# Attention and routing kernel: x read once into a ring of five batches, with the adds, zeros and one low half moved to match

## The chip, the cores and the metric

The kernel runs on one core of one Trainium2 chip. The metric is device time in microseconds (us), from start to end of one execution; less is better. The core has TensorE (PE, matrix products, with PEld for loading its weights), VectorE (DVE), ScalarE (ACT), GpSimd (POOL) and SyncE (SP), which here issues nearly all the DMAs, all on one queue. Each engine takes its instructions in order and waits on semaphores for the others.

## What is computed

16 batches of 1024 rows of 256 numbers are normalized; from these come an attention with a feature map (elu + 1) instead of a softmax and 16 heads, and a mixture of 8 experts in which each expert takes its 256 best rows of a batch. Both are added to x.

```python
x = L0_attn_x                       # 16 x 1024 x 256
xn = _layernorm(x, axis=-1)
# attention
Q = elu(xn @ Wq.T + bq) + 1;  K = elu(xn @ Wk.T + bk) + 1;  V = xn @ Wv.T + bv
KV = einsum('bshd,bshe->bhde', K, V)
Z = 1.0 / (einsum('bshd,bhd->bsh', Q, K.sum(axis=1)) + 1e-06)
out = einsum('bshd,bhde,bsh->bshe', Q, KV, Z).reshape(b, s, E) @ Wo.T + bo
# experts
probs = softmax(einsum('ntd,de->nte', xn, gate_w)).transpose(0, 2, 1)
g, m = jax.lax.top_k(probs, 256)
h = einsum('nekf,efd->nekd', gelu(einsum('nekd,edf->nekf', xn[m], w1)), w2)
ffn = zeros.at[m].add(g[..., None] * h).astype(bfloat16)
x = x + out + ffn
```

## The kernel before

The program has two parts. The first goes over the 16 batches: statistics, normalized rows, keys, queries, sums, the attention's output, and the gate. It leaves in memory the normalized rows in 16-bit halves (table), x plus attention (mix) and an array of zeros (acc) for the experts' sums. The second part gathers rows from table for each expert, multiplies by w1 and w2 and adds the results into acc; at its end acc is added to mix. The change touches the first part alone.

In the first part body n of each engine's program has eight slots, j = 0 to 7, one for each tile of 128 rows. In body n the keys and queries of batch n are made, and with a lag of two bodies (LAG) the output of batch m = n - 2.

- **SyncE** loads x of batch n + 2 into xring, which holds 3 batches (L601), and x of batch m + 1 a second time into x2ring, which holds 2 (L612). The second copy is where the output is summed. It also issues the DMA transposes of the normalized halves xhl into xT, one for each tile (turn, L558), of which tiles 4 to 7 of batch n and 0 to 3 of batch n + 1 are issued in body n; the rows for table (L569); the rows of mix (store_mix, L580); the weights that are scanned for their largest value (pieces, batches 2 to 9); and the zeros for acc (clear, L585), 16 of 1 MB, two in each of the bodies 8 to 15. A transpose waits for the low half of its tile.
- **VectorE** takes the statistics of x (L930), their moments for batch n + 1 in slot 3 (L946), the low halves of xhl (low, L1025), the feature map of the keys (k_feature, L1065), the reciprocals of Z and their splitting into three 16-bit parts (L1082 to L1092), the sum of output and x2ring (add_x, L1105), and in batches 5 to 15 the search for the 256 best of each expert (L254 to L262).
- **ScalarE** makes the high halves (L825), the exponentials and phk, the high half of the keys (key_high, L837).
- **GpSimd** makes, in this order in a slot: the centred tiles xm (centre, L733), phk's low half (key_low, L744) of the tile before, the bias bo added to two tiles of x2ring (add_bo, L759), in slots 1, 2, 5 and 6 for batch m. In slot 3 come the variance for batch n + 1 (norm, L722, after VectorE's moments), then key_low of tile 2 and the power -1/2 (root, L726), on which the centres of batch n + 1 depend. After the last body it has the adds of batches 14 and 15.
- **TensorE** projects a tile to its keys and logits (project, L1317 to L1322), sums keys times rows (sum_kv, L1335 and L1339, needs both halves of phk), projects the queries (L1356), makes denominators (L1368), spreads the reciprocals (L1389) and forms the output (L1404). In body 1 it multiplies the blocks of bv with Wo once (bias_blocks, L1307), from kvT, which VectorE writes at L1019.

The raw weights lie at the start in xring's third batch, and the raw bias of the keys in x2ring's second. The order is that in which each engine's program is written out; there is no scheduler.

## Time and profile before

| | us |
|---|---|
| median of three runs | 1897.31 |
| lowest, highest | 1896.3, 1904.78 |
| the profiled execution | 1902.01 |
| its span, first to last instruction | 1900.3 |

Mean granted clock of TensorE over the span: 0.990 of full speed. The first part ends, and the experts begin, at 545.73 us. The views are of one execution. The view by stretches gives for a stretch each engine's busy time with its number of instructions, the granted TensorE clock (1.00 is 2.4 GHz, 0.50 is 1.2 GHz), the share of the 16 DMA engines in use and the rate. A batch begins there where TensorE projects its first tile. In the timeline a row is an instruction or several alike: start, length, engine, line, operation, what it writes and reads, count, and in brackets the engine's idle time before it and what ended that.

### The profile page before, as it was taken

The page shows a single profiled execution, that of the slowest core. Times are in us where ns is not written, and L with a number is a line of the kernel's source. Part 1 is how long each engine was busy: PE and PEld are TensorE (multiplying, and loading weights), DVE is VectorE, ACT ScalarE, POOL GpSimd, SP SyncE. Part 2 cuts the span into 40 slices and gives each one's busy share as a digit, 9 for nine tenths or more (in the row PEclk, how much of TensorE's full clock was granted, in tenths as well). Part 3 has the DMA queues.
Part 4 walks back from the last instruction along what each step waited for, and adds up shares of the span by engine and source line. Part 5 has one row for each costly group of instructions (what it writes and reads, how often), then busy time and mean ns, then how long its engine had stood idle before and what let it go on. Part 6 is the DMA issues. An engine that isn't in the chain of part 4 may idle for free.

```text
span 1900.3 us, 39708 instructions
## 1 busy us (share of the span) xinstructions
PE 1836.1 (97%) x13916; PEld 1290.6 (68%) x13916; DVE 1294.9 (68%) x2569; ACT 1246.6 (66%) x2014; POOL 1104.5 (58%) x981
## 2 busy tenths in 40 slices
PE   5899998998999999999999999999999999999998
PEld 3577776776776666666666666666666666666666
DVE  6678997998857777745787875555555555555556
ACT  5788887776636666666666666666666666666665
POOL 6678786878535554655455555545554555555453
PEclk8999999999999999999999999999999999999999
DMA  6689899899755655575767667676766767676657
GB/s 167 165 238 257 238 249 265 227 255 236 206 166 124 131 122 120 139 187 143 172 151 187 154 159 181 134 179 157 185 155 158 172 137 184 154 186 156 179 124 222
DMA packets 449187, 338.26 MB, mean 178 GB/s; under 512 B 225043, under 2 KB 430614, under 8 KB 449046
## 3 DMA queue, kind: packets, MB, share of 16 engines
q1 hardware_dynamic: 383958, 253.84, 48.5%
q0 software_dynamic: 48864, 66.88, 19.4%
q10 hardware_dynamic: 16224, 15.73, 2.5%
q8 instruction: 79, 1.29, 0.3%
q14 instruction: 62, 0.51, 0.1%
HBM read 185.61 MB, written 100.40 MB: 151 GB/s over the span
## 4 chain that ended last, share of the span: by engine, by line
PE 70%; DMA 1%; DVE 0%; issue 0%; ACT 0%; POOL 0%; SPq 0%; POOLq 0%
PE pY L2005 35%; PE pH L1990 35%; DMA lacc<-acc 1%; DMA acc<-yo,idx 0%; PE pR L300 0%; POOL acc L1764 0%; ACT lffn L1800 0%; DVE yo L1866 0%; PE pN L240 0%; PE pN L284 0%; DVE lmix L1915 0%; DVE fffn L1912 0%; ACT hid L1789 0%; DVE hid L1850 0%; ACT gel L1786 0%
## 5 line engine op out<-in xcount | busy, mean ns | idle before, releaser
L2005 PE MATMUL pY<-w2s,hid 128*128 128x256 f16 x6144 | 756.6, 273 | 0.9 <-DVE hid L1850 0.8
L1990 PE MATMUL pH<-xgT,w1s 128*128 128x512 f16 (+1 forms) x3120 | 747.7, 376 | 1.3 <-PEq L329 1.3
L2005 PEld LDWEIGHTS pY<-w2s,hid 128*128 128x128 f16 x6144 | 599.7, 98 | 180.8 <-DVE yo L1866 3.6
L1764 POOL DMA_INDIRECT acc<-yo,idx x254 | 407.0, 1602 | 515.7 <-DVE yo L1866 442.7
L1850 DVE SCALAR_TENSOR_TENSOR hid<-gel,cur,hid 128x512 f16<-128x512 f32 (+1 forms) x520 | 384.6, 740 | 446.4 <-ACT hid L1789 345.5
L1786 ACT ACTIVATE gel<-pH,cur 128x512 f32<-128x512 f32 (+1 forms) x520 | 353.9, 681 | 481.5 <-PE pH L1990 405.7
L1990 PEld LDWEIGHTS pH<-xgT,w1s 128*128 128x128 f16 x3120 | 305.2, 98 | 252.3 <-DMA xgT<-xg 1.6
L1789 ACT ACTIVATE hid<-gel,cur 128x512 f16<-128x512 f32 (+1 forms) x520 | 372.0, 715 | 17.1
L224 POOL DMA_INDIRECT xg<-table,idx x256 | 292.3, 1142 | 112.1 <-issue 59.3
L733 POOL TENSOR_SCALAR xm<-xring,moments,rpow 128x256 f32<-128x256 f32 x128 | 163.9, 1281 | 2.0 <-DVE xhl L1025 0.4
L744 POOL TENSOR_TENSOR phk<-phik,phk 128x256 f16<-128x256 f32 x128 | 93.0, 727 | 108.6 <-ACT phk L837 107.4
L1866 DVE TENSOR_SCALAR yo<-pY,gains,cur 128x256 f32<-128x256 f32 x256 | 121.6, 537 | 14.6 <-PE pY L2005 13.0
L1339 PE MATMUL pKV<-phk,xhl 128*128 128x256 f16 x768 | 105.6, 275 | 0.0
L1356 PE MATMUL pQ<-xT,wq 128*128 128x512 f16 x384 | 94.2, 382 | 4.6 <-ACT qraw L844 4.5
L213 DVE SCALAR_TENSOR_TENSOR w1s<-stage,cur,w1s 128x1024 f16<-128x1024 f32 x64 | 83.0, 1296 | 17.8 <-ACT w1s L205 14.4
L213 DVE SCALAR_TENSOR_TENSOR w2s<-stage,cur,w2s 128x1024 f16<-128x1024 f32 x64 | 82.2, 1285 | 17.8 <-ACT w2s L205 12.9
L759 POOL TENSOR_TENSOR x2ring<-x2ring,bo_all 128x512 f32<-128x512 f32 x64 | 87.1, 1364 | 0.0
L825 ACT ACTIVATE xhl<-xm 128x256 f16<-128x256 f32 x128 | 52.5, 411 | 50.4 <-POOL xm L733 48.8
L1025 DVE TENSOR_TENSOR xhl<-xm,xhl 128x256 f16<-128x256 f32 x128 | 74.8, 585 | 6.4 <-ACT xhl L825 6.4
L830 ACT ACTIVATE ek<-pP,winv_neg 128x256 f32<-128x256 f32 x128 | 59.8, 467 | 25.4 <-PE pP L1322 25.2
L1317 PE MATMUL pP<-wkg,xT 128*128 128x272 f16 x256 | 52.0, 286 | 23.8 <-DMA xT<-xhl 16.6
L205 ACT ACTIVATE w1s<-stage,cur 128x1024 f16<-128x1024 f32 x64 | 72.5, 1133 | 0.0
(247 smaller groups left out, 1991.5 us busy)
## 6 DMA issues: line engine op xcount, KB each, us to landing
stage<-in_w SPq DMA_DIRECT2D x160, 512.0 KB, 5.0
xring<-in_x SPq DMA_DIRECT2D x16, 1024.0 KB, 7.1
x2ring<-in_x SPq DMA_DIRECT2D x16, 1024.0 KB, 7.8
table<-xhl SPq DMA_DIRECT2D x32, 512.0 KB, 4.7
mix<-x2ring SPq DMA_DIRECT2D x32, 512.0 KB
acc<-zeros SPq DMA_DIRECT2D x16, 1024.0 KB, 5.1
fmix<-mix SPq DMA_DIRECT2D x48, 256.0 KB
facc<-acc SPq DMA_DIRECT2D x48, 256.0 KB
```

The costliest lines, as they stand in the source:

```text
L213: nc.vector.scalar_tensor_tensor(out=part_dst(i, 1, r), in0=staged(r), scalar=cur[i][:, 2 + r // 2:3 + r // 2], in1=part_dst(i, 0, r), op0 ...
L224: nc.gpsimd.indirect_dma_start(xg[i][:, s, :, :, :].rearrange("p a c t -> p (a c t)"), None, table, bass.IndirectOffsetOnAxis(ap=idx[q % 4 ...
L733: g.tensor_scalar(xm[:, j % HALF, :], xring[:, n % XR, j, :], moments[:, j, 0:1], rpow[:, j:j + 1], ALU.subtract, ALU.mult).then_inc(xm_do ...
L1339: last = t.matmul(pKV[:, c * D:(c + 1) * D], xhl[h][:, jj, a, c, :], phk[:, j % 4, b, :], start=j == 0 and k == 0 and c == 0, stop=j == NT ...
L1356: last = t.matmul(pQ[:, :], wq[:, b, cc, c * P:(c + 1) * P], xT[h][:, a, cc, :], start=k == 0 and cc == 0, stop=k == 2 and cc == DC - 1)
L1764: g.indirect_dma_start(acc, bass.IndirectOffsetOnAxis(ap=idx[q][:, s:s + 1], axis=0), yo[i][:, s, :], None, compute_op=ALU.add).then_inc(a ...
L1786: a.activation(gel[:, hc % 2, w], pH[hc % 4][:, w], ACT.Gelu_apprx_tanh, scale=c[:, 0:1]).then_inc(gel_done, 1)
L1789: a.activation(hid[:, hc % 4, 0, w], gel[:, hc % 2, w], ACT.Copy, scale=c[:, 1:2]).then_inc(hhi_done, 1)
L1850: v.scalar_tensor_tensor(out=hid[:, hc % 4, 1, w], in0=gel[:, hc % 2, w], scalar=cur[expert_of(b, q)][:, 1:2], in1=hid[:, hc % 4, 0, w], o ...
L1866: last = v.tensor_scalar(yo[i][:, s, :], pY[s // 2][:, s % 2, :], gains[:, ds(column_of(b * 4 + quarter_of(b, q)) * 4 + s, 1)], cur[expert ...
L1990: last = t.matmul(pH[hc % 4][:, tok], w[:, aw, c, hc * P:(hc + 1) * P], xgT[i][:, ad, c, tok], start=k == 0 and c == 0, stop=k == 2 and c ...
L2005: last = t.matmul(pY[s // 2][:, s % 2, :], hid[:, hc % 4, ad, s * P:(s + 1) * P], w[:, aw, hc, :], start=hc == 0 and k == 0 and s % 2 == 0 ...
```

## The change

xring gets five batches and x2ring goes. Batch n lies in slot (n + 4) % 5, so that batch 15, which is stored in the second part, keeps the place that it had in memory. x is loaded once; the load of batch n + 2 stands after the transpose of tile 5, where the second load stood, and waits for the stored rows of batch n - 3. The bias is added in body n to batch n itself, two bodies earlier than before, in slots 2, 5, 6 and 7 instead of 1, 2, 5 and 6, and no adds stand behind the last body. The zeros of bodies 8 and 9 go to bodies 0 and 1. In slot 3 the low half of tile 2 stands ahead of the variance. The products of bv and Wo go from slot 0 to slot 4 of body 1 on TensorE (and from 1 to 5 on ScalarE), and the small constants of `offsets` from body 1 to body 3 on VectorE. Every line number behind the edits shifts by some lines, 5 to 10.

```diff
     LAG = 2
-    XR = 3
+    XR = 5
...
             xring = sb("xring", [P, XR, NT, D], F32)
-            x2ring = sb("x2ring", [P, 2, NT, D], F32)
+
+            def slot(n):
+
+                return (n + XR - 1) % XR
...
-                sp.dma_start(xring[:, 1, :, :], x_rows[1]).then_inc(x_in, 16)
-                sp.dma_start(x2ring[:, 0, :, :], x_rows[0]).then_inc(x2_in, 16)
+                sp.dma_start(xring[:, slot(1), :, :], x_rows[1]).then_inc(x_in, 16)
...
-                def body(n, s1, s2, load, load2, scan, ahead, wipe, nxt):
+                def body(n, s1, s2, load, scan, ahead, wipe, nxt):
                     m = n - LAG
                     if s1:
                         turn(n, HALF)
                         store_rows(n, 0)
+                    if s1:
+                        turn(n, HALF + 1)
                     if load:
                         value = held(sp, at(x_in, n, 1))
                         sp.wait_ge(consts, 1)
                         sp.wait_ge(x_in, value)
-                        value = held(sp, at(xm_done, n, -1))
-                        sp.wait_ge(consts, 1)
-                        sp.wait_ge(xm_done, value)
-                        sp.dma_start(xring[:, (n + 2) % XR, :, :], x_rows[ds(n + 2, 1)].rearrange("o p j d -> p (o j) d")).then_inc(x_in, 16)
-                    if s1:
-                        turn(n, HALF + 1)
-                    if load2:
-                        value = held(sp, at(x2_in, m))
-                        sp.wait_ge(consts, 1)
-                        sp.wait_ge(x2_in, value)
-                        for h in range(2):
-                            value = held(sp, at(mix_out[h], m, -1))
-                            sp.wait_ge(consts, 1)
-                            sp.wait_ge(mix_out[h], value)
-                        sp.dma_start(x2ring[:, ds((m + 1) % 2, 1), :, :].rearrange("p o j d -> p (o j) d"),
-                                     x_rows[ds(m + 1, 1)].rearrange("o p j d -> p (o j) d")).then_inc(x2_in, 16)
+                        if s2:
+                            for h in range(2):
+                                value = held(sp, at(mix_out[h], m, -1))
+                                sp.wait_ge(consts, 1)
+                                sp.wait_ge(mix_out[h], value)
+                        sp.dma_start(xring[:, ds(slot(n + 2), 1), :, :].rearrange("p o j d -> p (o j) d"),
+                                     x_rows[ds(n + 2, 1)].rearrange("o p j d -> p (o j) d")).then_inc(x_in, 16)
...
                     if wipe:
-                        clear(2 * n - NB)
+                        clear(2 * n if isinstance(n, int) and n < LAG else 2 * n - NB)
...
                 def add_bo(m, u):
 
-                    pool.wait_ge(x2_in, at(x2_in, m))
-                    tiles = x2ring[:, ds(m % 2, 1), 2 * u:2 * u + 2, :].rearrange("p o j d -> p (o j) d")
+                    pool.wait_ge(x_in, at(x_in, m))
+                    tiles = xring[:, slot(m), 2 * u:2 * u + 2, :]
...
-                        if nxt and j == HALF - 1:
-                            norm(n + 1)
                         if nxt and j > HALF:
                             centre(n + 1, j - (HALF - 1))
                         if j > 0:
                             key_low(n, j - 1)
                         elif n > 0:
                             key_low(n - 1, NT - 1)
                         if nxt and j == HALF - 1:
+                            norm(n + 1)
                             root(n + 1)
                         if nxt and j in (HALF - 1, HALF):
                             centre(n + 1, j - (HALF - 1))
-                        if n >= LAG and j in (1, 2, 5, 6):
-                            add_bo(n - LAG, (1, 2, 5, 6).index(j))
+                        if j in (2, 5, 6, 7):
+                            add_bo(n, (2, 5, 6, 7).index(j))
                         if n > 0 and j == HALF:
                             sums_of(n - 1)
                 key_low(NB - 1, NT - 1)
-                for u in range(4):
-                    add_bo(NB - LAG, u)
                 sums_of(NB - 1)
...
                 gather(pool, 0, 0, 0)
-                for u in range(4):
-                    add_bo(NB - 1, u)
...
-                    if n == 1:
+                    if n == LAG + 1:
                         offsets()
...
-                        if n == 1 and j == 0:
-                            bias_blocks()
                         if j in (2, 3):
                             q_part(n, j - 2)
+                        if n == 1 and j == 4:
+                            bias_blocks()
```

On SyncE, the stretch from the transpose of tile 4 in body 9: L601 is the load into xring, L612 the one into x2ring; before:

```order
L558 DMA_TRANSPOSE xT<-xhl 128x4x128
L569 DMA table<-xhl 128x4x512
L601 DMA xring<-in_x 128x8x256
L558 DMA_TRANSPOSE xT<-xhl 128x4x128
L612 DMA x2ring<-in_x 128x8x256
L558 DMA_TRANSPOSE xT<-xhl 128x4x128 x2
L569 DMA table<-xhl 128x4x512
L547 DMA stage<-in_w 128x1024
L547 DMA stage<-in_w 128x4x256
L558 DMA_TRANSPOSE xT<-xhl 128x4x128 x2
```

and now:

```order
L560 DMA_TRANSPOSE xT<-xhl 128x4x128
L571 DMA table<-xhl 128x4x512
L560 DMA_TRANSPOSE xT<-xhl 128x4x128
L607 DMA xring<-in_x 128x8x256
L560 DMA_TRANSPOSE xT<-xhl 128x4x128 x2
L571 DMA table<-xhl 128x4x512
L549 DMA stage<-in_w 128x1024
L549 DMA stage<-in_w 128x4x256
L560 DMA_TRANSPOSE xT<-xhl 128x4x128 x3
```

The load of x2ring is gone, and the one of xring (L607 now) stands behind the second transpose of the stretch, that of tile 5. The zeros (L585) that followed the transpose of tile 1 aren't in this body any more.

On SyncE the bodies 0 and 1, from the transposes of batch 1's tiles on, before:

```order
L558 DMA_TRANSPOSE xT<-xhl 128x4x128 x3
L569 DMA table<-xhl 128x4x512
L558 DMA_TRANSPOSE xT<-xhl 128x4x128 x5
L569 DMA table<-xhl 128x4x512
L601 DMA xring<-in_x 128x8x256
L558 DMA_TRANSPOSE xT<-xhl 128x4x128 x3
L569 DMA table<-xhl 128x4x512
L558 DMA_TRANSPOSE xT<-xhl 128x4x128 x4
L547 DMA stage<-in_w 128x1024
```

and now:

```order
L560 DMA_TRANSPOSE xT<-xhl 128x4x128 x2
L571 DMA table<-xhl 128x4x512
L560 DMA_TRANSPOSE xT<-xhl 128x4x128 x2
L587 DMA acc<-zeros 128x8x256
L560 DMA_TRANSPOSE xT<-xhl 128x4x128 x2
L587 DMA acc<-zeros 128x8x256
L560 DMA_TRANSPOSE xT<-xhl 128x4x128
L571 DMA table<-xhl 128x4x512
L560 DMA_TRANSPOSE xT<-xhl 128x4x128
L607 DMA xring<-in_x 128x8x256
```

The zeros (acc, L587 now) stand between transposes of batches 1 and 2.

On GpSimd, slots 0 to 3 of a body from batch 2 on. xm is a centred tile, phk a low half of the keys, veps the variance, rpow the power; before:

```order
L733 TENSOR_SCALAR xm<-xring,moments,rpow 128x256
L744 TENSOR_TENSOR phk<-phik,phk 128x256
L733 TENSOR_SCALAR xm<-xring,moments,rpow 128x256
L744 TENSOR_TENSOR phk<-phik,phk 128x256
L759 TENSOR_TENSOR x2ring<-x2ring,bo_all 128x512
L733 TENSOR_SCALAR xm<-xring,moments,rpow 128x256
L744 TENSOR_TENSOR phk<-phik,phk 128x256
L759 TENSOR_TENSOR x2ring<-x2ring,bo_all 128x512
L722 TENSOR_SCALAR veps<-moments 128x8
L744 TENSOR_TENSOR phk<-phik,phk 128x256
L726 TENSOR_TENSOR rpow<-veps,minus_half 128x8
L733 TENSOR_SCALAR xm<-xring,moments,rpow 128x256
```

and now:

```order
L754 TENSOR_TENSOR xring<-xring,bo_all 128x512
L728 TENSOR_SCALAR xm<-xring,moments,rpow 128x256
L739 TENSOR_TENSOR phk<-phik,phk 128x256
L728 TENSOR_SCALAR xm<-xring,moments,rpow 128x256
L739 TENSOR_TENSOR phk<-phik,phk 128x256
L728 TENSOR_SCALAR xm<-xring,moments,rpow 128x256
L739 TENSOR_TENSOR phk<-phik,phk 128x256
L754 TENSOR_TENSOR xring<-xring,bo_all 128x512
L739 TENSOR_TENSOR phk<-phik,phk 128x256
L717 TENSOR_SCALAR veps<-moments 128x8
L721 TENSOR_TENSOR rpow<-veps,minus_half 128x8
L728 TENSOR_SCALAR xm<-xring,moments,rpow 128x256
```

An add has gone from slot 1 to the end of the body before, ahead of the low half of the last tile there, and in slot 3 the low half of tile 2 stands ahead of the variance.

## Rows read from the trace of the kernel before

**Rows 1.** The page: busy time and share of each engine; a group of instructions.
```profile
PE 1836.1 (97%) x13916; PEld 1290.6 (68%) x13916; DVE 1294.9 (68%) x2569; ACT 1246.6 (66%) x2014; POOL 1104.5 (58%) x981
...
L759 POOL TENSOR_TENSOR x2ring<-x2ring,bo_all 128x512 f32<-128x512 f32 x64 | 87.1, 1364 | 0.0
```
**Rows 2.** Stretches, from:to length, then PE, PEld, DVE, ACT, POOL busy, clock, DMA.
```profile
44.05:75.96 31.91, 22.53 (x167) 14.92 (x165) 17.08 (x64) 22.32 (x51) 19.01 (x21) 0.89 0.40 102
...
137.01:166.28 29.27, 29.27 (x289) 23.24 (x288) 23.74 (x60) 25.52 (x57) 23.30 (x24) 1.00 0.88 251
...
196.95:227.11 30.16, 29.19 (x285) 22.55 (x284) 28.16 (x74) 25.66 (x57) 24.13 (x24) 1.00 0.92 245
...
287.43:324.77 37.34, 32.18 (x286) 24.30 (x284) 28.06 (x75) 25.88 (x57) 23.49 (x24) 0.91 0.93 257
...
385.21:417.56 32.35, 29.77 (x287) 22.77 (x286) 30.30 (x84) 21.71 (x48) 25.07 (x24) 1.00 1.04 235
...
448.34:480.88 32.54, 29.18 (x286) 22.54 (x285) 27.00 (x70) 21.85 (x48) 23.87 (x24) 1.00 0.94 260
...
509.80:545.73 35.93, 30.62 (x281) 25.32 (x281) 23.01 (x47) 3.29 (x7) 15.41 (x17) 0.86 0.34 103
545.73:1900.30 1354.57, 1346.39 (x9328) 914.10 (x9328) 850.49 (x1390) 858.16 (x1168) 711.85 (x571) 1.00 0.66 160
...
515.80:526.00 10.20, 8.99 (x66) 7.29 (x67) 5.72 (x10) 0.00 (x0) 0.00 (x0) 0.50 0.46 156
```
**Rows 3.** TensorE's waits from 80 to 500 us: in total, times, longest.
```profile
PE pP L1317 <- DMA xT<-xhl: 13.6, 10, 2.7
PE pS L1335 <- POOL phk L744: 8.3, 9, 1.0
```
**Rows 4.** Timeline of SyncE's queue in batch 9 (the two loads of x).
```profile
296.05 0.42 SPq L601 DMA_DIRECT2D xring<-in_x  x1
...
299.16 0.40 SPq L612 DMA_DIRECT2D x2ring<-in_x  x1
299.66 5.88 SPq L558 DMA_TRANSPOSE xT<-xhl  x2
```
**Rows 5.** The page's DMA issues: count, size of each, median us to landing.
```profile
xring<-in_x SPq DMA_DIRECT2D x16, 1024.0 KB, 7.1
x2ring<-in_x SPq DMA_DIRECT2D x16, 1024.0 KB, 7.8
...
acc<-zeros SPq DMA_DIRECT2D x16, 1024.0 KB, 5.1
```
**Rows 6.** Timeline of TensorE in batch 9, the projection of tile 6.
```profile
308.67 0.64 PE L1317 MATMUL pP<-wkg,xT 128*128 128x272 f16 x2 [2.72 <-DMA xT<-xhl]
```
**Rows 7.** Timeline of GpSimd in batch 8, slots 0 and 3.
```profile
260.07 0.67 POOL L744 TENSOR_TENSOR phk<-phik,phk 128x256 f16<-128x256 f32 x1 [3.82 <-ACT phk L837]
...
269.38 0.81 POOL L722 TENSOR_SCALAR veps<-moments 128x8 f32<-128x8 f32 x1 [1.36 <-DVE moments L946]
270.27 0.67 POOL L744 TENSOR_TENSOR phk<-phik,phk 128x256 f16<-128x256 f32 x1
```
**Rows 8.** Timeline in batch 1: VectorE's kvT and TensorE's products with it.
```profile
48.03 0.47 DVE L1019 TENSOR_SCALAR kvT<-head_mask,bvT 128x128 f32<-128x128 f32 x2
...
48.56 0.80 PE L1307 MATMUL pD<-woT,kvT 128*128 128x256 f32 x1 [3.56 <-DVE kvT L1019]
```
**Rows 9.** Timeline in the tail, GpSimd, VectorE and TensorE.
```profile
510.22 4.99 POOL L759 TENSOR_TENSOR x2ring<-x2ring,bo_all 128x512 f32<-128x512 f32 x4
...
512.83 1.26 DVE L1088 TENSOR_TENSOR zrest<-zz,zpart 128x128 f32<-128x128 f32 x1
514.12 1.17 DVE L1090 CAST zpart<-zrest 128x128 bf16<-128x128 f32 x1
...
516.60 0.80 PE L1420 MATMUL pP<-woT,kvT 128*128 128x256 f32 x1 [3.21 <-DVE kvT L1070]
...
529.58 0.36 DVE L1088 TENSOR_TENSOR zrest<-zz,zpart 128x128 f32<-128x128 f32 x1
```

47 lines of the change are left out of this document (23 added, 24 removed).

## The prediction

> **What bounds the kernel now.** I read the views in this order: busy time, stretches between batch starts, waits, and the timeline of what stands around each wait. TensorE is busy for 97% of the span [rows 1]. The stretches show two parts. From 545.73 us to the end are the experts: TensorE is busy for 1346.39 of 1354.57 us there at full clock [rows 2], and no edited instruction stands there, so I take its time as fixed. The edits all lie in the 545.73 us before it, the attention part, 16 batches long.
>
> In batch 4 (137.01 to 166.28) TensorE is busy for all 29.27 us: that is TensorE's own work for a batch, the floor. Batches 2 to 14 reach from 75.96 to 480.88, 404.92 us for 13 batches, and 13 floors are 380.5. So 24.4 us stand above the floor. Three things fill them: waits of the K projection (L1317) for a transpose from the DMA queue, 13.6 us in 10 waits; waits of the K sums (L1335) for GpSimd's low half phk, 8.3 us in 9 [rows 3]; and batch 9, where TensorE was busy for 32.18 us at a granted clock of 0.91 against 29.2 elsewhere [rows 2], 3.0 us for a stretch at 1.2 GHz after its waits. The sum, 24.9, agrees with 24.4. Batch 1 and the tail (509.80 to 545.73) have losses of their own. VectorE is nearly as full: 28.16 of 30.16 us in batch 6 [rows 2].
>
> **The loads of x.** The change takes out 16 loads of 1 MB, as many as it keeps; the kept ones take 7.1 us from issue to landing, the removed 7.8 [rows 5]. Before, the queue of batch 9 held load, transpose 5, second load, transposes 6 and 7, the two loads 3.1 us apart [rows 4]: 2 MB are asked for in 3 us and need some 11. Transpose 6 is issued right behind the second load and its projection waited 2.72 us [rows 6]. Now transpose 5 goes ahead of the one load that is left, and transpose 6 stands behind 1 MB instead of 2. The load takes the place of the second one, about 3 us later than the first was issued, so transpose 6 lands about 7.4 (what a load takes) minus 3.1 = 4 us earlier relative to its projection. The largest wait is 2.72, so nearly all ten go. Two exceptions: zeros now go out in batches 0 and 1, two of their transfers (5.1 us each, [rows 5]) just before batch 2, which has a wait of this kind; and batch 14 has four weight loads ahead of a transpose, untouched by the change. For the two I keep 3 us. Bounds for the term: 0 (below) and 13.6; taken 10.6. Batches 8 and 9 also lose their four zero writes, which collided there with loads and the scan, so the low clock of batch 9 goes: 3.0, all or nothing.
>
> The x load now also waits for the stored rows of the batch three back. SP waited for that in the same place before, for the second load, so nothing new is queued behind it. VectorE wants this x only in slot 7, five slots of some 3.7 us later (29.3 us have eight), and the load takes 7.1 [rows 5]: cost 0, and it would need a delay of over 10 us to cost anything.
>
> **The third tile's low half.** In batch 8, GpSimd waited for VectorE's moments until 269.38, did the variance and only then the low half at 270.27 to 270.94, for which TensorE was waiting [rows 7]. With the low half first it runs about 1.2 us earlier, since its input was there; the wait for moments moves behind it, where the next centre stands, and this has slots of slack because the next batch's first transposes land long before use. TensorE's 8.3 us go. What is late next is VectorE: at a period of 29.27 its 28.16 us leave 1.1 us for its own waits, where it had 2.0 [rows 2]. Bounds 0 and 8.3; I take 6, nearer the upper end because batch 4 ran at the floor with VectorE and GpSimd in the same order [rows 2].
>
> **The bias adds.** 64 adds of 1.36 us stay 64. In the steady batches three stand about where they were; the fourth goes from the second slot to the end of the batch before, ahead of the low half of tile 7. GpSimd sat idle for 3.82 us just before that one [rows 7], which covers 1.4; cost 0 there, 1.4 a batch if that cover were gone. Removing it from slot 1 frees nothing that is waited for. The eight adds of batches 0 and 1, new there, are 10.9 us of GpSimd work beside TensorE's; batch 1 leaves it 31.91 - 19.01 = 12.9 us idle [rows 2]. Bounds: 0 and some 4 if they push the centres; taken 1.
>
> **The head.** In batch 1 TensorE waited 3.56 us for kvT, which VectorE wrote only at 48.03 behind the offsets and statistics, and then did the four products at half clock [rows 8]. The products go four slots later and the offsets two batches on, so the wait goes. Batch 1 is a chain of short waits of all engines (TensorE 22.53 of 31.91 busy), so part is given back: bounds 1 and 5.5, taken 4. The zeros now go through the queue here, at a DMA share of 0.40 [rows 2]; four transfers of 5.1 us in front of transposes: bounds 0 and 10, taken 1.
>
> **The tail.** Before, four adds (510.22 to 515.21) ran on GpSimd while VectorE split the reciprocals: one step took 1.26 us and the next 1.17, where the first took 0.36 later with GpSimd quiet. TensorE waited 3.21 us behind them [rows 9]. These adds are gone from here: 2.0 us (bounds 1 and 2.2). The Trainium skill, "SBUF — State Buffer", section "Who interferes with whom", says that a VectorE instruction with two SBUF inputs and a GpSimd one that reads SBUF block each other for a whole instruction; by this rule the step grew by waiting for an add, and the trace agrees. Then the clock: 515.80 to 526.00 ran at 0.50, 1.2 GHz, with TensorE busy for 8.99 us [rows 2]; half of that, 4.5, comes back if it doesn't fall. With the wait down to about 1.2 us it is like batch 12, whose waits left the clock at 1.00 [rows 2], more than like batch 9. Bounds 0 and 4.5, taken 3 since VectorE's chain runs beside it. The four adds at the very end lay behind TensorE's work: 0.
>
> **The sum.** 10.6 + 3.0 + 6 + 4 + 2 + 3 = 28.6 saved, 2 spent: 26.6. The profiled execution took 1902.0 us (its span 1900.3 and 1.7 around it), 4.7 above the median of the runs, 1897.3. From 1902.0 the sum gives 1875.4; from the median 1870.7. Part of the 4.7 will be waits of the kind that go, part not: I take 1873.
>
> **The rivals.**
> 1. VectorE becomes the bound. For it: 28.16 of 30.16 us busy in batch 6, 30.30 in batch 12. Against: half of VectorE's 2.0 us of idle time is enough for the floor. If the period stays near 30.1 in the nine batches 5 to 13, the 6 us are not gained and some 3 of the DMA term: 1873 + 9 = 1882. The Trainium skill's page "SBUF — State Buffer", by the rule above, gives it a reason: adds that have moved by a slot or two meet other two-input steps of VectorE. What that would give is this same case.
> 2. The wait changes its name: transpose 6 still stands behind a load, and if this is late because SP comes to it late, the term of 10.6 and the 3.0 stay: 1873 + 13.6 = 1887. Against: 4 us of relief against waits of at most 2.72.
> 3. All goes: upper bounds throughout (13.6 + 3 + 8.3 + 5.5 + 2.2 + 4.5 = 37) and less than nothing spent: 1862.
> 4. Slower. The four zero writes ahead of transposes in batches 0 to 2 each hold a projection for their 5.1 us, and TensorE falls to 1.2 GHz after each, 3 us a time as in batch 9: 32 us, against a gain that is cut to 20 because batch 1's goes too: 1897 + 12 = 1909. It decides from the point where those transposes have under 5 us of slack. Against: a DMA share of 0.40 in batch 1.
>
> **Chances.** Forecast (1866 to 1880) 0.56; rival 1 0.17; rival 2 0.12; rival 3 0.09; rival 4 0.06. A measurement here can tell about 0.5% from no change, which is 9.5 us: faster is below 1887.8. Forecast, rivals 1 and 3 and part of rival 2 lie there: 0.83; within 0.11, slower 0.06. The range from 1862 to 1889 leaves out rival 4, the far side of rivals 2 and 3, and no more.
>
> **What would show it.** In the profile of the changed kernel: waits of L1317's successor for xT below 4 us in 80 to 500 us, no wait of the K sums for phk, batches 6 to 8 at 29.3 to 29.6 us, batch 9 no longer than its neighbours, the products of the bias with no wait in batch 1, the reciprocal's splitting step at 0.36 us in the tail and a clock of 1.00 after it, and the start of the experts near 519 us. If batches 6 to 8 still take 30 us, VectorE was the bound; if batches 0 to 2 have grown, the zeros or the early adds cost more than I allowed; if the experts' part moves by more than 1 us, my first step was wrong.

## The result and the profile after

The changed kernel takes 1883.74 us (median of 4 runs, 1881.06 to 1884.64), the kernel before 1899.3 (4 runs, the three of "Time and profile before" and one more). The ratio is 0.9913 with a 95% interval from 0.9886 to 0.9939. It is faster. The time lies in the range of 1862 to 1889 us, but outside the 1866 to 1880 to which the forecast itself gave 0.56, and nearest to rival 1's 1882. The gain is 15.6 us in the medians. In the profiled executions, from which the sum was made, it is 18.7 us where the sum gave 26.6: the span went from 1900.3 to 1881.6 us.

The stretches of the changed kernel answer to [rows 2]. The columns are the same: from:to, length, then the busy time of TensorE, its weight loads, VectorE, ScalarE and GpSimd, the granted clock, the DMA share and GB/s. In order: batches 0 and 1, batches 6, 7, 9 and 14, batch 15 with the tail, batches 2 to 14 together, the experts, and 6.8 us in batch 1. The last line is batches 2 to 14 of the kernel before.

```profile
19.41:75.00 55.59, 41.90 (x305) 27.14 (x306) 32.90 (x91) 41.58 (x94) 45.26 (x45) 0.84 0.72 176
...
193.00:222.61 29.61, 29.18 (x286) 22.54 (x285) 27.77 (x74) 25.49 (x57) 24.17 (x25) 1.00 0.74 213
222.61:252.54 29.93, 29.34 (x286) 22.38 (x284) 28.07 (x75) 25.43 (x58) 24.72 (x25) 1.00 0.82 212
282.47:312.90 30.43, 29.32 (x286) 22.56 (x284) 28.51 (x76) 25.63 (x58) 25.45 (x25) 1.00 0.80 211
...
434.62:468.18 33.56, 30.74 (x286) 23.50 (x285) 27.63 (x72) 21.60 (x48) 24.70 (x25) 0.95 0.85 231
468.18:526.84 58.66, 55.30 (x565) 44.77 (x564) 46.05 (x103) 27.56 (x55) 22.66 (x25) 1.00 0.49 144
75.00:468.18 393.18, 381.63 (x3702) 295.13 (x3700) 348.95 (x936) 311.88 (x690) 315.37 (x313) 1.00 0.81 211
...
526.84:1881.60 1354.76, 1346.38 (x9328) 914.11 (x9328) 851.36 (x1390) 858.00 (x1168) 710.66 (x571) 1.00 0.66 160
67.50:74.30 6.80, 4.03 (x19) 2.00 (x20) 3.68 (x9) 4.69 (x9) 6.27 (x7) 0.50 0.64 186
...
75.96:480.88 404.92, 382.64 (x3702) 296.31 (x3700) 352.39 (x923) 313.83 (x689) 310.90 (x312) 0.99 0.93 247
```

Laid beside the kernel before, stage by stage (us; the third column is what the prediction's terms make of the first):

| stage | before | after | by the prediction |
|---|---|---|---|
| up to batch 0 | 19.8 | 19.4 | 19.8 |
| batches 0 and 1 | 56.2 | 55.6 | 54.2 |
| batches 2 to 14 | 404.9 | 393.2 | 385.3 |
| batch 15 and the tail | 64.9 | 58.7 | 59.9 |
| experts | 1354.6 | 1354.8 | 1354.6 |

The missing 7.9 us lie in batches 2 to 14; batches 0 and 1 fell short by 1.4 more, and the tail and the start made that up. In batches 2 to 14 TensorE's idle time went from 22.3 to 11.6 us (length less busy time), which is 10.7 less where 16.6 was forecast, and its busy time fell by 1.0 instead of 3.0. The two shortfalls, 5.9 and 2.0, are the 7.9. The waits of TensorE there, and those of the first 80 us (what it waited for; total, times, longest), the former to be read beside [rows 3]:

```profile
PE pP L1307 <- DMA xT<-xhl: 5.4, 3, 2.5
PE pS L1325 <- POOL phk L739: 3.6, 8, 0.6
PE pP L1307 <- DVE phik L1055: 2.6, 7, 0.8
```

```profile
PE pQ L1346 <- ACT qraw L834: 8.2, 3, 4.2
```

The waits for transposes fell from 13.6 us to 5.4, and two make up nearly all of that: batch 2 (2.06) and batch 14 (2.51). The waits for the low half phk fell from 8.3 us to 3.6 in 8, not to nothing, and a wait for VectorE's phik that stood at 0.3 is now 2.6. Against the forecast these are 2.4, 1.3 and 2.3 us, together the 6 us of idle time that did not go. The other 2.0 is the clock: batch 9's busy time fell by 2.9 us (32.18 in [rows 2], now 29.32), but batch 14's rose by 1.6 (29.18 and 30.74), at a granted clock of 0.95. In the first 80 us a wait for the queries, qraw, takes 8.2 us. The loads of x land sooner than in [rows 5]:

```profile
xring<-in_x SPq DMA_DIRECT2D x16, 1024.0 KB, 6.0
```

### The profile page after: what moved, and what is told of

Same layout as the page of the kernel before. It is cut to its first block and busy times, and to the rows that moved or that the text cites. A ratio compares the mean times of both kernels' runs of the same rounds, so it can differ in the third digit from the quotient of the medians.

```text
span 1881.6 us, 39627 instructions
## 1 busy us (share of the span) xinstructions
PE 1829.9 (97%) x13916; PEld 1285.1 (68%) x13916; DVE 1289.9 (69%) x2569; ACT 1243.8 (66%) x2014; POOL 1108.2 (59%) x981
## 5 line engine op out<-in xcount | busy, mean ns | idle before, releaser
L739 POOL TENSOR_TENSOR phk<-phik,phk 128x256 f16<-128x256 f32 x128 | 100.0, 781 | 96.5 <-ACT phk L827 96.0
L754 POOL TENSOR_TENSOR xring<-xring,bo_all 128x512 f32<-128x512 f32 x64 | 89.8, 1403 | 0.0
L205 ACT ACTIVATE w2s<-stage,cur 128x1024 f16<-128x1024 f32 x64 | 72.5, 1132 | 0.0
```

The costliest lines, as they stand in the source:

```text
L205: nc.scalar.activation(part_dst(i, 0, r), staged(r), ACT.Copy, scale=cur[i][:, 2 + r // 2:3 + r // 2]).then_inc(whi_done, 1)
```

## The experiments

Each kernel below is the changed kernel with the named edit. The table gives the median and, from the profiled execution, four stages in us, each from one batch's first projection to that of another: batches 0 to 2, 3 to 13, 14, and 15 with the tail up to the experts. The experts take 1354.4 to 1357.1 us in all of them. The kernel before took 1899.55, 1900.1 and 1899.7 us in the three sessions, beside 1899.3 with the changed kernel, so medians of different sessions can be laid side by side to about 1 us. The stages are of one execution each. It lies within 2 us of the kernel's median, but for the kernel before (2.7 above), e5 (1889.56 us, 3.3 above) and e8 (1875.56, 4.3 below). Of the intervals only that of e12 lies clear of the changed kernel's; those of e2, e6, e8 and e10 overlap it, so their gains of 3 to 5 us over the changed kernel are not known to 1 us.

| kernel | median | ratio to before, 95% | 0 to 2 | 3 to 13 | 14 | 15, tail |
|---|---|---|---|---|---|---|
| before | 1899.3 | | 87.7 | 340.8 | 32.5 | 64.9 |
| changed kernel | 1883.74 | 0.9913 [0.9886, 0.9939] | 86.7 | 328.6 | 33.6 | 58.7 |
| e1 ring alone | 1888.89 | 0.9944 [0.9927, 0.996] | 85.3 | 333.1 | 32.1 | 62.0 |
| e2 variance back | 1878.49 | 0.99 [0.9878, 0.9922] | 85.3 | 327.5 | 30.9 | 58.6 |
| e3 zeros back | 1883.56 | 0.9922 [0.9902, 0.9943] | 82.9 | 331.2 | 33.2 | 58.6 |
| e4 adds back | 1887.5 | 0.994 [0.9922, 0.9959] | 82.5 | 333.0 | 33.7 | 62.0 |
| e5 head back | 1886.22 | 0.9925 [0.9904, 0.9947] | 93.2 | 328.6 | 33.5 | 58.2 |
| e6 early adds out | 1880.39 | 0.9897 [0.9873, 0.9921] | 84.1 | 329.5 | 32.8 | 58.2 |
| e7 adds in the tail | 1885.5, one run | | 85.0 | 328.6 | 33.5 | 62.1 |
| e8 adds spread | 1879.83 | 0.9902 [0.9883, 0.9921] | 82.1 | 327.8 | 31.1 | 58.6 |
| e9 queries later | 1885.45 | 0.9929 [0.9907, 0.995] | 88.6 | 329.2 | 33.0 | 58.6 |
| e10 stage loads later | 1878.68 | 0.989 [0.9867, 0.9914] | 85.9 | 328.9 | 30.2 | 58.2 |
| e11 e2 and e8 | 1876.63 | 0.9875 [0.9853, 0.9897] | 85.2 | 326.8 | 31.6 | 58.2 |
| e12 e2, e8 and e10 | 1873.89 | 0.9861 [0.9839, 0.9882] | 84.7 | 326.6 | 29.7 | 58.2 |

**e1: the ring alone.** Everything but the ring of five slots and the single load of x is undone: the variance, the adds, the zeros and the head stand where they stood before. The lines for the zeros and the bias's products are those shown under e3 and e5.

```diff
             for j in range(NT):
...
+                if nxt and j == HALF - 1:
+                    norm(n + 1)
...
-                    norm(n + 1)
...
-                if j in (2, 5, 6, 7):
-                    add_bo(n, (2, 5, 6, 7).index(j))
+                if n >= LAG and j in (1, 2, 5, 6):
+                    add_bo(n - LAG, (1, 2, 5, 6).index(j))
...
+            for u in range(4):
+                add_bo(NB - LAG, u)
...
+            for u in range(4):
+                add_bo(NB - 1, u)
...
-                if n == LAG + 1:
+                if n == 1:
                     offsets()
...
```

> The kernel before with the ring of five and the single load of x alone: adds, zeros, order of the low half and head products where they were. Theory (half of the transposes' waits come from the second load in the queue): batches 2 to 14 fall from 404.9 us to about 396, the batch with scan and zeros together from 37.3 to about 33, and the waits for xT from 13.6 us to about 6; batches 0 and 1 stay at 56 us and the tail (from TensorE's first tile of batch 15 to the experts) at 64.9. Total about 9 us under the kernel before. Rival (the loads weren't the cause, the wait changes its name): batches 2 to 14 stay within 3 us of 404.9.

Measured: 1888.89 us, 10.7 less than before. Batches 2 to 14 went from 404.9 to 394.2, also 10.7. The profiled execution is 13.8 us shorter; the other 3 lie in the tail (62.0 instead of 64.9), where none had been expected. Batch 9 went from 37.34 to 32.24 with the clock at 1.00, although its zeros were still there. In the columns of [rows 2], here are batch 7, batch 9 and batch 15 with the tail, and TensorE's waits from 80 to 484 us:

```profile
222.67:252.82 30.15, 29.18 (x285) 22.65 (x284) 28.43 (x75) 25.63 (x57) 24.14 (x24) 1.00 0.82 210
282.97:315.21 32.24, 29.39 (x286) 22.49 (x284) 28.45 (x75) 25.75 (x57) 23.75 (x24) 1.00 0.98 266
...
469.77:531.73 61.96, 56.68 (x565) 46.00 (x564) 49.47 (x103) 27.56 (x55) 32.31 (x33) 0.97 0.46 136
```

```profile
PE pS L1330 <- POOL phk L739: 8.2, 9, 1.0
PE pP L1312 <- DMA xT<-xhl: 4.8, 2, 3.0
```

The ring carries two thirds of the gain of the whole change. The waits for transposes fell from 13.6 to 4.8, those for phk stayed at 8.2. So the two kinds of wait are separate, and rival 2, by which transpose 6 stays late and the whole term is lost, falls.

**e2: the variance ahead again.** Only the third tile's low half goes back behind the variance.

```diff
+                if nxt and j == HALF - 1:
+                    norm(n + 1)
...
                     key_low(n - 1, NT - 1)
                 if nxt and j == HALF - 1:
-                    norm(n + 1)
                     root(n + 1)
```

> The changed kernel with the variance ahead of tile 2's low half again. Theory (the move gained some 0.4 us a batch where the search for the best runs, since the low half then met VectorE's two-input steps and kept 0.4 to 0.6 us of TensorE's wait): batches 2 to 14 grow from 393.2 us by 4 to 6, TensorE's waits for phk from 3.6 to about 8 us, total 4 to 6 us over the changed kernel. Rival (VectorE is the bound in these batches, so that the wait is free): no change beyond 1 us.

Measured: 1878.49 us, 5.2 under the changed kernel in the median, where 4 to 6 more had been expected. The intervals overlap: that the move, priced at 6 us of gain, gained nothing is surer than that it lost 5. The timeline of GpSimd (start, duration, operation, idle time before it) and of TensorE and VectorE in batch 7 of the changed kernel shows what took its place:

```profile
234.38 1.48 POOL L739 TENSOR_TENSOR phk<-phik,phk 128x256 f16<-128x256 f32 x1 [1.16 <-ACT phk L827]
235.95 0.20 POOL L717 TENSOR_SCALAR veps<-moments 128x8 f32<-128x8 f32 x1
```

```profile
234.34 0.38 DVE L1015 TENSOR_TENSOR xhl<-xm,xhl 128x256 f16<-128x256 f32 x1
234.66 0.67 DVE L1047 TENSOR_TENSOR qring<-qraw,eq 128x512 f32<-128x512 f32 x1
```

```profile
235.92 0.25 PE L1325 MATMUL pS<-one_col,phk 128*128 128x1 f16 x4 [0.59 <-POOL phk L739]
```

And GpSimd and TensorE in batch 7 of e2, with e2's waits from 80 to 484 us:

```profile
234.18 0.67 POOL L739 TENSOR_TENSOR phk<-phik,phk 128x256 f16<-128x256 f32 x1
```

```profile
234.91 0.25 PE L1326 MATMUL pS<-one_col,phk 128*128 128x1 f16 x4 [0.81 <-POOL phk L739]
```

```profile
PE pS L1326 <- POOL phk L739: 5.0, 8, 0.8
PE pP L1308 <- DVE phik L1056: 1.2, 3, 0.6
```

The low half now starts before the variance, but takes 1.48 us instead of the 0.67 of [rows 7], while VectorE does two steps with two inputs from SBUF, the on-chip memory, each; TensorE waits 0.59 us, against 0.81 in e2. In the kernel before the stretched operation was the variance (0.81 in [rows 7], 0.20 here), and the low half behind it was short. GpSimd and VectorE stand in each other's way in this place in both orders. The move only chose who pays. From 80 to 484 us it took 1.4 us from the waits for phk (5.0 to 3.6) and added 1.4 to those for phik (1.2 to 2.6); what makes phik late no run shows. With e1 and e4 this gives batch 7 in four forms, all at full clock (head and zeros, in which e1 and e4 also differ, have no work in batch 7):

| batch 7, us | adds in slots 1, 2, 5, 6 | adds in slots 2, 5, 6, 7 |
|---|---|---|
| variance ahead of the low half | 30.15 (e1) | 29.82 (e2) |
| low half ahead of the variance | 30.27 (e4) | 29.93 (changed) |

```profile
221.53:251.35 29.82, 29.02 (x286) 22.68 (x285) 28.09 (x75) 25.64 (x57) 24.35 (x25) 1.00 0.78 212
```

```profile
220.56:250.83 30.27, 29.49 (x286) 22.40 (x285) 28.42 (x75) 25.43 (x58) 24.66 (x24) 1.00 0.75 209
```

In both columns the new order of low half and variance costs 0.1 us a batch; in both rows the new place of the adds gains 0.33 or 0.34. Over batches 3 to 13 the order costs 1.0 us (327.5 against 328.6). The rest of e2's lead in the profile lies in batches 0 to 2 (1.3 us, within what two executions of the same order differ by there, see the end) and in batch 14 (2.7 us). Batch 14 waits for its transpose in either kernel, but in the changed one the clock falls behind this wait (0.95) and in e2 it doesn't. That is not one execution's luck alone: of the kernels with the stage's loads in their old place the three with the variance ahead (e1, e2, e11) kept the clock at 1.00 there, and of the eight with the other order seven fell to 0.95 (all but e8). What in the order decides this no run shows.

**e4: the adds back.** The bias adds go back to two batches later, in slots 1, 2, 5 and 6 and in the tail.

```diff
-                if j in (2, 5, 6, 7):
-                    add_bo(n, (2, 5, 6, 7).index(j))
+                if n >= LAG and j in (1, 2, 5, 6):
+                    add_bo(n - LAG, (1, 2, 5, 6).index(j))
...
             key_low(NB - 1, NT - 1)
+            for u in range(4):
+                add_bo(NB - LAG, u)
...
+            for u in range(4):
+                add_bo(NB - 1, u)
```

> The changed kernel with the bias adds back at a lag of two batches, in slots 1, 2, 5 and 6 and behind the last body. Theory (the early adds hold up a centre, with it ScalarE's queue and the queries, and TensorE's clock falls): batches 0 and 1 together fall from 55.6 us to about 48, TensorE has no wait of 4 us for qraw there; the tail grows from 58.7 us to about 63, with a splitting step over 1 us and the clock at half after it. Total about the same as the changed kernel, within 4 us. Rival (zeros in the queue are what lengthened batches 0 and 1): batches 0 and 1 stay at 55 us and only the tail grows, total 4 to 6 us slower than the changed kernel.

Measured: 1887.5 us, 3.8 above the changed kernel. Three parts with different signs: batches 0 to 2 are 4.2 us shorter, batches 3 to 13 4.5 longer, the tail 3.3 longer. Batches 0 and 1 fell to 51.4 us, not to 48. The adds cost where they are early and gain in the tail as forecast, and the gain in the steady batches was not in the prediction at all.

**e6: the early adds left out.** It shows the price of the early adds with nothing put in their place; bo is missing from batches 0 and 1 of its output.

```diff
-                if j in (2, 5, 6, 7):
+                if n >= LAG and j in (2, 5, 6, 7):
                     add_bo(n, (2, 5, 6, 7).index(j))
...
-                    dve.wait_ge(bo_done, at(bo_done, m, u))
+                    if m >= LAG:
+                        dve.wait_ge(bo_done, at(bo_done, m - LAG, u))
```

> The changed kernel without the eight bias adds of batches 0 and 1 (bo is left out of these two batches of the output). Theory (early adds): batches 0 and 1 fall from 55.6 us to about 48, nothing else moves, total about 7 us under the changed kernel. Rival (zeros): no change beyond 1 us.

Measured: 1880.39 us, 3.3 less than the changed kernel, half of the 7 that had been expected. Batches 0 and 1 take 50.2 us instead of 55.6; half of that is given back in batch 2 (33.8 us instead of 31.1), where the projection of tile 6 waits 3.18 us for its transpose and the clock falls. In the changed kernel, GpSimd, ScalarE and TensorE in batch 0 look like this:

```profile
37.40 1.45 POOL L754 TENSOR_TENSOR xring<-xring,bo_all 128x512 f32<-128x512 f32 x1
38.84 1.39 POOL L728 TENSOR_SCALAR xm<-xring,moments,rpow 128x256 f32<-128x256 f32 x1
```

```profile
40.26 0.42 ACT L815 ACTIVATE xhl<-xm 128x256 f16<-128x256 f32 x1 [2.06 <-POOL xm L728]
...
41.24 0.77 ACT L834 ACTIVATE qraw<-pQ,bqT_one,winv 128x512 f32<-128x512 f32 x1
```

```profile
42.07 2.74 PE L1346 MATMUL pQ<-xT,wq 128*128 128x512 f16 x6 [3.91 <-ACT qraw L834]
```

The add at 37.40 stands ahead of the centre at 38.84. ScalarE's high half, which needs that centre, waits 2.06 us, the queries stand behind it on ScalarE, and TensorE waits 3.91 us for them, then does the next six products in 2.74 us at half clock (e2's take 1.47 at the same place). The same happened at 70.28 in batch 1, with a wait of 4.17. Not all of this is the adds' doing. Counted from the first projection of batch 0, the queries start after 22.7 us here and 22.5 in e2, which has the same adds, and after 21.5 in e6: an add makes them about 1 us later. In e2 the clock did not fall there, and batches 0 and 1 took 51.6 us. The prediction had seen GpSimd's idle time in batch 1 and not the order inside it.

**e7: adds in the tail.** Four adds of the same size, on data of their own, run on GpSimd where the old ones ran; the rest stays.

```diff
                 key_low(NB - 1, NT - 1)
+                mo_in = spread[:, 0:4, :, :].rearrange("p j c t -> p (j c t)").bitcast(F32).rearrange("p (i d) -> p i d", i=2)
+                for u in range(4):
+                    if u >= 1:
+                        pool.wait_ge(extra_done, at(extra_done, 0, u - 1))
+                    g.tensor_tensor(extra[:, :, :], mo_in, bo_all[:, :].unsqueeze(1).to_broadcast([P, 2, D]), ALU.add).then_inc(extra_done, 1)
```

> The changed kernel with four adds of the same size on GpSimd, of other data into a scratch tile, put back behind the last body, ahead of ksz. Theory (an add and a step of VectorE with two inputs in the on-chip memory hold each other up, and the longer wait of TensorE drops its clock): the steps of splitting take over 1 us instead of 0.3, TensorE waits about 3 us for kvT, the granted clock is 0.5 for 5 to 10 us after it, and the tail grows from 58.7 us by 4 to 6. Rival (the tail gained by the shorter batch 15 alone): the tail grows by less than 1 us.

Measured: 1885.5 us in one run; batch 15 and the tail take 62.1 us instead of 58.7, 3.4 more where 4 to 6 had been expected. VectorE and TensorE in its tail:

```profile
499.13 1.37 DVE L1085 TENSOR_TENSOR zrest<-zz,zpart 128x128 f32<-128x128 f32 x1
500.54 1.24 DVE L1087 CAST zpart<-zrest 128x128 bf16<-128x128 f32 x1
```

```profile
503.09 2.08 PE L1417 MATMUL pP<-woT,kvT 128*128 128x256 f32 x4 [3.52 <-DVE kvT L1067]
```

And in the changed kernel, where the adds are gone:

```profile
499.90 0.29 DVE L1078 TENSOR_TENSOR zrest<-zz,zpart 128x128 f32<-128x128 f32 x1
500.22 0.23 DVE L1080 CAST zpart<-zrest 128x128 bf16<-128x128 f32 x1
```

```profile
501.76 1.13 PE L1410 MATMUL pP<-woT,kvT 128*128 128x256 f32 x4 [1.07 <-DVE kvT L1060]
```

The step zrest takes 1.37 us with the adds beside it and 0.29 without, the cast behind it 1.24 and 0.23, and TensorE waits 3.52 and 1.07 us, as in [rows 9] and as the prediction had it. The Trainium skill, "SBUF — State Buffer", section "Who interferes with whom", says that copies and casts of VectorE, where their operands allow a mode with two ports, can contend with GpSimd as well as steps with two inputs do; the cast's 1.24 against 0.23 us agrees.

**e9: the queries later.** VectorE's q_feature of tile 0 goes from slot 3 to slot 4, away from the third tile's low half. This takes one of the two steps with two inputs out of its way.

```diff
-                if j in (3, 4):
-                    q_feature(n, j - 3)
+                if j == 4:
+                    q_feature(n, 0)
+                    q_feature(n, 1)
```

> The changed kernel with VectorE's first query feature (two inputs in the on-chip memory) one slot later, so that it isn't running when GpSimd makes the low half of tile 2. Theory (the two hold each other up): the low half of tile 2 takes 0.7 to 1.0 us instead of 1.5 in batches 6 to 13, TensorE's wait for it falls from 0.6 to 0.1 us, and batches 6, 7, 8 and 10 come down from 29.6 to 29.9 us to about 29.2, total 2 to 4 us less. Rival (the low half is slow for another reason, or VectorE is the bound): no change beyond 1 us.

Measured: 1885.45 us, 1.7 above the changed kernel where 2 to 4 less had been expected (its batches 0 to 2 are 1.9 us longer), but the place in question changed as the block between the two engines says. GpSimd in batch 7, and the batch:

```profile
238.69 0.88 POOL L739 TENSOR_TENSOR phk<-phik,phk 128x256 f16<-128x256 f32 x1 [1.17 <-ACT phk L827]
```

```profile
227.03:256.58 29.55, 29.20 (x285) 22.39 (x284) 28.04 (x76) 25.33 (x58) 24.09 (x25) 1.00 0.80 214
```

The low half took 0.88 us instead of 1.48, no wait for phk was left in that batch, and batches 6 to 8 took 29.55 to 29.67 us, the upper end of the 29.3 to 29.6 of the prediction; 29.2 had been expected of this run. Over 80 to 484 us the wait for phk is 0.9 us in 1 instead of 3.6 in 8. VectorE had the same work (28.04 us busy), in less time: its load was not the bound, the collision was. The two query steps then stand in a row, with a phik behind them, and that wait grew from 2.6 to 4.3 us:

```profile
PE pP L1308 <- DMA xT<-xhl: 6.7, 4, 2.4
PE pP L1308 <- DVE phik L1055: 4.3, 8, 1.4
PE pS L1326 <- POOL phk L739: 0.9, 1, 0.9
```

The sum of the three waits in this view is 11.9 us, and 11.6 in the changed kernel. The wait for phk fell by 2.7 us, those for phik and for transposes grew by 1.7 and 1.3. This is rival 1's mechanism, by a narrower path than it was written.

**e3: the zeros back.** The four zero writes of batches 0 and 1 go back to batches 8 and 9.

```diff
-                        (0, 1, True, False, True, False, False, True),
-                        (1, LAG, True, False, True, False, True, True),
+                        (0, 1, True, False, True, False, False, False),
+                        (1, LAG, True, False, True, False, True, False),
...
-                        (PIECE_NB, PIECE_NB + 1, True, True, True, True, True, False),
-                        (PIECE_NB + 1, PIECE_NB + SCAN0, True, True, True, True, False, False),
+                        (PIECE_NB, PIECE_NB + 1, True, True, True, True, True, True),
+                        (PIECE_NB + 1, PIECE_NB + SCAN0, True, True, True, True, False, True),
```

> The changed kernel with the four transfers of zeros back in bodies 8 and 9. Theory (zeros cost little in batches 0 and 1 and most of the gain of batch 9 is theirs): batches 0 and 1 shrink by 0 to 1 us, batch 2 by 1 to 2, batch 9 grows from 30.4 by 2 to 4 us; total 0 to 3 us over the changed kernel. Rival (zeros are what lengthened batches 0 and 1): these shrink by 5 us or more and the total falls.

Measured: 1883.56 us, 0.2 off the changed kernel. Batch 2 and batch 9:

```profile
73.47:102.30 28.83, 28.83 (x286) 22.80 (x284) 22.28 (x60) 25.00 (x56) 23.48 (x25) 1.00 0.84 204
278.38:312.08 33.70, 30.96 (x285) 23.57 (x284) 27.90 (x76) 25.70 (x58) 24.98 (x25) 0.95 0.96 254
```

Batch 2 is 2.2 us shorter (28.83 against 31.1), batch 9 3.3 us longer (33.70 against 30.43) with the clock at 0.95. The zeros collide with transposes where they are written, here or there. As stages, batches 0 to 2 are 3.8 us shorter and batches 3 to 13 2.6 longer. The 1.5 us of this that lie in batches 0 and 1 are within what two executions of the same order differ by there. The move of the zeros is worth nothing in the median.

**e5: the head back.** The bias's blocks and products and the offsets go back to the start of batch 1.

```diff
-                        if j == 5 and n == 1:
+                        if j == 1 and n == 1:
                             bias_blocks_out()
...
-                if n == LAG + 1:
+                if n == 1:
                     offsets()
...
+                        if n == 1 and j == 0:
+                            bias_blocks()
                         if j in (2, 3):
                             q_part(n, j - 2)
-                        if n == 1 and j == 4:
-                            bias_blocks()
```

> The changed kernel with its head undone alone: the bias's blocks, their products, their copies and the offsets go back from batches 1 and 3 to the start of batch 1. The step on record gave this 4 us (1 to 5.5). The changed kernel took 55.6 us for batches 0 and 1 and the kernel with the ring alone 56.2, so the gain was not to be seen; with the early adds back at their old place it was (51.4). Theory: the head's gain and the early adds' cost are separate and add up. Then batches 0 and 1 take 59 to 61 us here and the time is 1887 to 1889 us. Rival: in batches 0 and 1 the late queries behind the early adds end last, whatever the bias's products do before them, so the head hides in that wait: batches 0 and 1 at 55 to 57 us, and the time within 1.5 us of the changed kernel's 1883.7.

Measured: 1886.22 us. Batches 0 and 1 take 59.7 us, 4.1 more than in the changed kernel; with batch 2, where the clock falls too, it is 6.5 more. Batches 0 and 1 also take 3.5 us more than in e1 (56.2), which has the same head and no early adds (and no early zeros). That agrees with the theory that head and early adds are separate and add up in that stage; the rival, that the head hides in the wait for queries, falls. In the median the difference is 2.5 us and the intervals of the two kernels overlap, and the profiled execution is the slowest of its four, so the size is known only as 2.5 to 6.5.

**e8: the adds spread.** The twelve adds of batches 0 to 2 go behind the centres, into other slots, from slot 2 of batch 0 to slot 0 of batch 3.

```diff
+                early = {(0, 2): (0, 0), (1, 0): (0, 1), (1, 1): (0, 2), (1, 2): (0, 3), (1, 7): (1, 0),
+                         (2, 0): (1, 1), (2, 1): (1, 2), (2, 2): (1, 3), (2, 5): (2, 0), (2, 6): (2, 1),
+                         (2, 7): (2, 2), (3, 0): (2, 3)}
...
+                        if j < 2 and (n, j) in early:
+                            add_bo(*early[n, j])
...
-                        if j in (2, 5, 6, 7):
+                        if n > LAG and j in (2, 5, 6, 7):
                             add_bo(n, (2, 5, 6, 7).index(j))
+                        elif n <= LAG and j >= 2 and (n, j) in early:
+                            add_bo(*early[n, j])
```

> The changed kernel with the adds of batches 0 and 1 spread over bodies 0 to 3, where GpSimd waits anyway ahead of the low halves, and none ahead of the centres of slots 6 and 7 in bodies 0 and 1; all else equal. Theory (early adds ahead of a centre are the cost): batches 0 and 1 fall from 55.6 us to about 50, total 4 to 6 us under the changed kernel. Rival (GpSimd has too little idle time for eight more adds anywhere there): batch 2 or 3 grows by what batches 0 and 1 lose, and the total stays.

Measured: 1879.83 us, 3.9 less than the changed kernel, and batches 0 to 2 take 82.1 us instead of 86.7. All adds are done, and this stage is as short as with the adds at their old place (e4, 82.5) or left out (e6, 84.1): the price was their place, not their time on GpSimd. How large it is a pair of profiles does not say. The changed kernel's is the longest of the three with its order in this stage (86.7; e10 85.9, e7 85.0), and their mean is 3.0 us above that of e4, e6 and e8. With the variance ahead there is hardly a difference: 85.3 with the early adds (e2), 85.2 and 84.7 with the adds spread (e11 and e12 below).

**e10: the stage's loads later.** The four weight loads go behind the last transpose of batch 14.

```diff
                         store_rows(n, 1)
+                    if isinstance(n, int) and n == NB - 2:
+                        for r in range(4):
+                            sp.dma_start(staged(r), part_src(0, r)).then_inc(part_in[r], 16)
...
                             for q in range(PIECES):
                                 sp.wait_ge(piece_done[q], at(piece_done[q], PIECE_NB - 1))
-                            for r in range(4):
-                                sp.dma_start(staged(r), part_src(0, r)).then_inc(part_in[r], 16)
```

> The changed kernel with one edit: the four loads of the stage (2 MB), which are issued at the head of batch 14 ahead of its transposes, are issued behind the transpose of tile 7 of that batch. Theory: these loads hold up the transpose of tile 4, which landed 8.7 us after its issue and made TensorE wait 2.5 us and fall to half its clock; batch 14, 33.6 us in the changed kernel, comes to 30.5 to 31 us, no other batch gets longer, and the time is 1880 to 1881.5 us. Rival: the same 2 MB meet the next transposes instead (tiles 0 to 3 of batch 15, issued behind them), and the wait moves there: batch 14 as short, but batch 15 or the tail longer by 2 to 3 us, the time within 1 us of 1883.7.

Measured: 1878.68 us, 5.1 less than the changed kernel. SyncE's queue in batch 14 of the changed kernel, the wait behind it, and then the same place in e10 with its batch 14 and its tail:

```profile
436.86 3.66 SPq L657 DMA_DIRECT2D stage<-in_w  x4
440.68 3.28 SPq L560 DMA_TRANSPOSE xT<-xhl  x1
```

```profile
449.39 0.41 PE L1307 MATMUL pP<-wkg,xT 128*128 128x272 f16 x2 [2.51 <-DMA xT<-xhl]
```

```profile
437.92 2.09 SPq L560 DMA_TRANSPOSE xT<-xhl  x1
...
449.06 2.87 SPq L615 DMA_DIRECT2D stage<-in_w  x4
```

```profile
434.36:464.60 30.24, 29.36 (x285) 22.39 (x284) 27.60 (x72) 21.51 (x48) 24.43 (x25) 1.00 0.99 247
464.60:522.85 58.25, 55.09 (x566) 44.71 (x565) 46.03 (x104) 27.57 (x55) 23.70 (x26) 1.00 0.51 152
```

The transpose of tile 4 is issued at 437.92 instead of 440.68 (the batches start within 0.3 us of each other), its wait is gone, batch 14 takes 30.24 us instead of 33.56, and the tail is no longer. The rival, that the loads only meet the next transposes, falls. The profile shows 3.3 us of the 5.1.

**e11 and e12: the gains together.** e11 is the changed kernel with the variance back (e2) and the adds spread (e8); e12 has the stage's loads later (e10) as well. Their diffs are those above.

> The changed kernel with two edits that gained apart: the variance stands ahead of the third tile's low half again (1878.5 us alone), and the early adds of batches 0 to 2 are spread out behind the centres and over more tiles (1879.8 alone). Theory: the two are separate, one in GpSimd's order once a batch, the other in GpSimd's order at the start, and their gains add up: 1874 to 1876 us. Rival: what either gained lay in batches 0 and 1 (51.6 and 51.5 us instead of 55.6), where TensorE's low clock after a wait made most of the price, and it can be gained only once: batches 0 and 1 at 51 us again and the time 1878 to 1880 us.

Measured: 1876.63 us, 1.9 under e2 and 3.2 under e8. Batches 0 and 1 take 51.4 us, as in either kernel alone, so what was gained there is gained once, as the rival had it. Batch 2 is 33.8 us long as in e2 (e8: 30.6), again a wait with a fall of the clock. Only batches 3 to 13 gain by both. The median lies between the two forecasts and the intervals of the three kernels overlap: neither is confirmed.

> The kernel with the variance back and the early adds spread, and with the stage's four loads behind the last transpose of batch 14. Theory: the stage's loads cost 2 to 3 us in batch 14 whatever stands at the start, so this is 2 to 3 us under the kernel without this edit: 1872 to 1874 us. Rival: without a wait in batch 14 the gain is what a dip of the clock cost by chance (batch 14 took 30.9 and 31.1 us in the kernels with either edit alone, against 33.6), and this is within 1 us of the kernel without it.

Measured: 1873.89 us, 2.7 less than e11, of which the theory forecast 2 to 3. Batch 14:

```profile
431.32:460.99 29.67, 29.01 (x286) 22.71 (x285) 26.93 (x71) 21.73 (x48) 24.14 (x25) 1.00 0.94 241
```

This kernel takes 0.9861 of the time before, interval 0.9839 to 0.9882, and its experts start at 519.23 us. It is the fastest of all that ran, 9.8 us under the changed kernel's median. The interval lies wholly below that of the changed kernel (0.9886 to 0.9939).

## Why the prediction was right, and where it was not

The direction held, and so did the way to it in its first step: the experts' part moved by 0.2 us, and all of the gain lies in the attention part. The range held too, but partly by luck: it was wide enough to cover rivals 1 and 2, and a gain of 4.5 us that the prediction put at nothing stands against terms that failed. The forecast time of 1873 was 10.7 us too low. 7.9 of these are the stages of the table; 2.4 come from the base, since the sum from the profiled execution gave 1875.4 and I went below it; the remaining 0.4 is the distance of the changed kernel's profiled execution (1883.36) from its median. Term by term:

**The loads of x: the mechanism right, the term too large.** The waits for transposes went as forecast, and the ring alone gives 10.7 us (e1). The prediction gave 10.6 for the waits and 3.0 for batch 9's clock, 13.6 together. The clock of batch 9 it put down to the zeros, but the ring brought it to 1.00 with the zeros still there (e1), while the zeros beside the new order brought it back to 0.95 (e3). It took 10.6 of the 13.6 us of waits as gone; 8.8 went in e1 and 8.2 in the changed kernel. I had kept 3 us for batches 2 and 14; they came to 4.6, with a fall of the clock (0.95) in batch 14 on top. In batch 14 the cause is the four stage loads, which the prediction named and did not price (e10: 3.3 us in the profile, 5.1 in the median). In batch 2 it is the zeros.

**The third tile's low half: the step that failed.** It was priced at 6 us because "its input was there". The input was, but VectorE's two steps stand at the same moment, and the low half took 1.48 us instead of 0.67. Against e2 the move took 1.4 us from TensorE's waits for phk, where 6 was priced, and gave as much to those for phik, which was in no term; it loses 1.0 us over batches 3 to 13, and 5.2 in the median, of which 2.7 in the profile hang on the clock in batch 14. Of the fall of the waits for phk from 8.2 (e1) to 3.6, 1.4 to 2.4 us are the move's and 2.2 to 3.2 the adds', by the order in which e2 and e4 are put between the two. The row was on the table: the variance took 0.81 us in [rows 7]. I had read the tail's stretched step as a block between the engines, and did not ask the same of this one. The comparison with batch 4 was no evidence, for batch 4's VectorE had 23.74 us of work and batch 6's 28.16 [rows 2].

**The bias adds in the steady batches: a gain that was put at nothing.** "Removing it from slot 1 frees nothing that is waited for" is wrong by 0.34 us a batch, as the table of four forms shows in both rows, and by 4.5 us over batches 3 to 13 (e4). TensorE's waits for phk are 5.8 us in e4 and 3.6 in the changed kernel, which differ in the adds alone, and 8.2 and 5.0 in e1 and e2, between which the head and the zeros move too. That the add in slot 1 makes the next centre later, and so the moments for which GpSimd waits in slot 3, is the likely way; no run shows it.

**Batches 0 to 2: the signs were right, the sizes were off.** The ring brings this stage from 87.7 to 85.3 us (e1). The head gains 4.1 us in batches 0 and 1 and 6.5 with batch 2 (e5; 2.5 in the median); 4 was forecast. The early adds cost 4.2 (e4), 2.6 (e6) and 4.5 (e8) in the stage, about 3 over several profiles (see e8), and 3.3 and 3.9 in the medians of e6 and e8; 1 was forecast, with 4 as the bound. The zeros cost 3.8 there (e3), 2.2 of it in batch 2; 1 was forecast, with 10 as the bound. With 1.3 for the order of low half and variance (e2), 85.3 - 6.5 + 4.2 + 3.8 + 1.3 = 88.1 us, where 86.7 was measured. Single profiles are no better than that in this stage, so the parts add up only roughly. The mistake with the adds was to compare their 10.9 us with the idle time of a whole batch. What decides is what stands behind an add in GpSimd's own order: a centre, and behind that ScalarE's queries. What the zeros cost here they gain in batches 8 and 9, 2.6 us, so that rival 4 had its mechanism right in one batch (batch 2) and not in four places.

**The tail: right, and a little more.** 5 us forecast, 6.2 in the profile. The adds account for 3.3 and 3.4 of it (e4 and e7, each with the clock at 0.97 in that stage). The rest is clock, and no run shows its cause: e1, with the adds in the tail and TensorE's wait for kvT at 3.20 us as in [rows 9], took 62.0 us with TensorE busy for 56.68, where the kernel before took 64.9 with 59.54. So the 6.2 owe 2.9 to how long the low clock lasted in the profile of the kernel before. The 0.36 us of [rows 9] was not taken with GpSimd quiet, as the prediction says, but while it issued gathers; with GpSimd quiet the step takes 0.29.

**The rivals.** The time came out nearest to rival 1's 1882. Its condition, a period near 30.1 us in batches 5 to 13, was met (30.05 on average), and for a reason that it named in its last sentences: moved work met steps of VectorE, though it was the low half and not the adds. But VectorE wasn't the bound by its load. It was idle for 1.9 us in a batch of 29.93, and e9 ran the same work in 29.55.

**The signs.** Of those I had given, these came true: no wait of the bias's products, the splitting step (0.29 us) and the clock in the tail, and the experts' part. These did not: waits for transposes under 4 us (5.4), no wait for phk (3.6), batches 6 to 8 at 29.3 to 29.6 us (29.6, 29.9, 29.9), batch 9 no longer than its neighbours (30.43 against 29.93 and 29.60), and the start of the experts near 519 us (526.8). e12 reaches that last one at 519.23, with the low half back at its old place.

## What to carry to other kernels

When an operation is moved to where its engine is idle, look at what the neighbour on the same memory ports does at that moment, and at what stands behind it in its own engine's order. Idle time summed over a batch answers neither. A wait that goes is worth its own length only if the next one isn't a fraction of a microsecond behind; here the low half's wait fell and phik's rose by half as much. And when a queue is cleared of one large transfer, read what else stands ahead of the same consumers, since moving four loads that the change had left alone gave as much as any single part but the ring.

## What the runs showed of the hardware

**GpSimd and VectorE hold each other up for whole instructions, in either direction.** The low half took 0.67 us in [rows 7], 0.88 with one such step of VectorE beside it (e9) and 1.48 with two in a row; VectorE's zrest took 0.29 or 1.37, its cast 0.23 or 1.24. The low half ended 0.53 us after the end of VectorE's last such step in the changed kernel, 0.54 in e9 and 0.53 in e4 (batch 7 each), though it had started 0.95, 0.34 and 1.04 us before that end. So it did most of its work only when the steps beside it were over.

**The same order of work does not take the same time in every execution.** Batches 0 and 1 are alike in the changed kernel, in e10 (first line) and in e7 (second):

```profile
19.64:74.57 54.93, 41.22 (x305) 26.88 (x305) 32.79 (x91) 41.68 (x94) 45.32 (x45) 0.88 0.76 178
```

```profile
19.92:72.42 52.50, 41.30 (x305) 27.67 (x306) 30.79 (x87) 40.95 (x92) 43.52 (x44) 0.93 0.81 184
```

They took 55.59, 54.93 and 52.50 us at a granted clock of 0.84, 0.88 and 0.93. In this stage TensorE waits often, and which stretch after a wait is run at 1.2 GHz differs from one profile to the next: in the changed kernel it was also 67.5 to 74.3 us, where TensorE was busy for 4.03 of 6.80 us at 0.50. What is won is partly lost again: counted to the end of batch 2 the three took 86.7, 85.9 and 85.0 us, since an earlier start of batch 2 only lengthens its wait for the transpose behind the zeros (2.06, 1.92 and 3.50 us). So differences of up to 3 us in batches 0 and 1, and up to 2 us to the end of batch 2, say nothing between two single profiles.
